# Attention and gated FFN in one kernel: the weighted-value products of a group's second half in the next group's first step, a seventh probsT slot, task 2 after the fourth tile's scores

## The reference, cut to what matters

```python
qkv = jnp.einsum('bsd,ed->bse', x, w_qkv) + b_qkv
scores = jnp.einsum('bhqd,bhkd->bhqk', q, k) / math.sqrt(Hd)     # Hd = 32
attn = jax.nn.softmax(scores + causal[None, None], axis=-1)
out = jnp.einsum('bhqk,bhkd->bhqd', attn, v)
x = _layernorm(x + jnp.einsum('bsd,ed->bse', out, w_out) + b_out)
h = jax.nn.silu(g) * u        # g, u: products with (gate_w - 128) * scale, (up_w - 128) * scale
x = _layernorm(x + jnp.einsum('bsi,hi->bsh', h, Wd))
```

## Time and profile before

| what | us |
|---|---|
| median of 3 runs (lowest, highest) | 754.64 (753.57, 755.45) |
| the profiled execution | 754.66 |
| its span, first to last instruction | 752.6 |
| PE, PEld, DVE, ACT, POOL busy | 730.2, 563.9, 392.5, 381.4, 135.5 |
| groups 0 and earlier, to 47.66 | PE busy 43.30 |
| FFN, 388.90 to 752.60 | PE busy 354.15 of 363.70 |

### The profile page before, as it was taken

The page is one execution under the profiler, slowest core; times in us unless marked ns, Lnnn a source line. Parts: engine busy times, 40 slices in busy tenths (PEclk is TensorE's granted clock), DMA queues, the critical chain, the costliest instruction groups (busy, mean ns, idle before and its releaser), DMA issues.

```text
span 752.6 us, 11957 instructions
## 1 busy us (share of the span) xinstructions
PE 730.2 (97%) x4480; PEld 563.9 (75%) x4480; DVE 392.5 (52%) x1004; ACT 381.4 (51%) x912; POOL 135.5 (18%) x154
## 2 busy tenths in 40 slices
PE   7999899999999999999899999999999999999994
PEld 6776576776777777776588888888888888888883
DVE  4756665666666665676653222643227332453335
ACT  3656766667766667766656555322223232322220
POOL 0010110304313061311816212230000000000003
PEclk9999999999999999999999999999999999999998
DMA  9201413334613355221587974541110010000201
GB/s 314 106 2 29 141 57 84 84 86 92 189 57 85 84 139 155 63 67 57 99 166 159 196 223 139 169 147 50 70 57 0 14 73 24 0 1 28 84 1 57
DMA packets 59463, 68.67 MB, mean 91 GB/s; under 512 B 33552, under 2 KB 35600, under 8 KB 59280
## 3 DMA queue, kind: packets, MB, share of 16 engines
q1 hardware_dynamic: 52880, 48.00, 21.3%
q0 software_dynamic: 6528, 19.93, 11.5%
HBM read 59.53 MB, written 14.68 MB: 99 GB/s over the span
## 4 chain that ended last, share of the span: by engine, by line
PE 89%; DVE 5%; ACT 4%; POOL 1%; issue 1%; DMA 1%; POOLq 0%; SPq 0%; DVEq 0%
PE bank L1438 15%; PE bank L1439 15%; PE bank L1220 12%; PE bank L1296 9%; PE bank L1445 7%; PE bank L1446 7%; PE bank L1235 6%; PE bank L1279 5%; PE bank L1317 5%; PE bank L1254 4%; ACT probs L757 2%; DVE probs L973 2%; PE bank L1328 1%; PE bank L1182 1%; ACT xT_hi L750 1%; PE bank L1192 1%
## 5 line engine op out<-in xcount | busy, mean ns | idle before, releaser
L757 ACT ACTIVATE probs<-probs,neg_max 128x128 f32<-128x128 f32 (+3 forms) x256 | 140.4, 552 | 12.0 <-DVE neg_max L973 11.9
L1089 DVE SCALAR_TENSOR_TENSOR hid<-bank,u_scale,silu 128x512 f32<-128x512 f32 x64 | 48.0, 750 | 164.3 <-PE bank L1439 163.1
L973 DVE CUSTOM_DVE_ANT_0 probs<-bank,causal 128x128 f32<-128x128 f32 (+3 forms) x256 | 111.6, 484 | 32.6 <-PE bank L1279 32.6
L1438 PE MATMUL bank<-xT_hi,gateT 128*128 128x512 f32 x256 | 100.3, 392 | 0.0
L1439 PE MATMUL bank<-xT_lo,gateT 128*128 128x512 f32 x256 | 99.7, 389 | 0.0
L1438 PE MATMUL bank<-xT_hi,upT 128*128 128x512 f32 x256 | 99.6, 389 | 0.0
L1439 PE MATMUL bank<-xT_lo,upT 128*128 128x512 f32 x256 | 99.6, 389 | 0.0
L865 ACT ACTIVATE silu<-bank,g_scale 128x512 f32<-128x512 f32 x64 | 44.0, 688 | 96.8 <-PE bank L1439 96.8
L1296 PEld LDWEIGHTS bank<-ident,probs 128*128 128x128 f32 x640 | 72.4, 140 | 27.1 <-issue 14.4
L871 ACT ACTIVATE hid_hi<-hid 128x512 fp32r<-128x512 f32 x58 | 36.7, 632 | 108.9 <-DVE hid L1089 108.9
L1445 PE MATMUL bank<-downT,hid_hi 128*128 128x512 f32 x232 | 90.3, 389 | 0.1
(11 more groups left out here) (102 smaller groups left out, 1185.6 us busy)
## 6 DMA issues: line engine op xcount, KB each, us to landing
scan_buf<-in_L_ffn_gate_w_dram SPq DMA_DIRECT2D x4, 1024.0 KB, 5.4
scan_buf<-in_L_ffn_up_w_dram SPq DMA_DIRECT2D x4, 1024.0 KB, 5.2
scan_buf<-in_L_ffn_down_w_dram SPq DMA_DIRECT2D x4, 1024.0 KB, 5.3
x_tok<-y_scratch SPq DMA_DIRECT2D x4, 1024.0 KB, 5.7
w_int<-in_L_ffn_gate_w_dram POOLq DMA_DIRECT2D x16, 256.0 KB, 3.4
w_int<-in_L_ffn_up_w_dram POOLq DMA_DIRECT2D x16, 256.0 KB, 3.1
w_int<-in_L_ffn_down_w_dram POOLq DMA_DIRECT2D x16, 256.0 KB, 3.9
z_tok<-y_scratch SPq DMA_DIRECT2D x4, 1024.0 KB, 5.7
```

What stands on the lines that cost most here:

```text
L757: nc.scalar.activation(probs[qb][:, j, :], probs[qb][:, j, :], ACT.Exp, bias=neg_max[:, qb, j:j + 1], scale=-1.0, accum_out=row_sum[:, qb, ...
L973: nc.vector.tensor_tensor_reduce(out=probs[qb][:, j, :], in0=score[j][:, first:first + w], in1=causal[:, S - w:S], scale=-SCALE, scalar=-F ...
L1089: nc.vector.scalar_tensor_tensor(out=hid[:, i % 2, :], in0=bank[:, :], scalar=u_scale[:, i:i + 1], in1=silu[:, i % 2, :], op0=ALU.mult, op ...
L1438: nc.tensor.matmul(acc[n][:, :], w[:, c, cols], form(xT_hi[:, c, :]), start=c == 0, stop=False)
```

## The change

Three numbers of two tables, and one size:

```diff
-    TASK_STEPS = [0, 0, 2, 8, 8, 10, 10, 12, 12, 15]
+    TASK_STEPS = [0, 0, 3, 8, 8, 10, 10, 12, 12, 15]
...
-    PRODUCT_STEPS = [8, 8, 12, 12, STEPS, STEPS]
+    PRODUCT_STEPS = [8, 8, STEPS, STEPS, STEPS, STEPS]
...
-    SLOTS = 6
+    SLOTS = 7
```

## The result

| what | before | after |
|---|---|---|
| median of 6 runs (lowest, highest), us | 755.03 (753.48, 755.45) | 748.67 (748.46, 749.80) |
| the profiled execution | 754.66 | 748.73 |
| its span | 752.6 | 746.8 |
| FFN, from its first product to the end | 363.7 | 363.7 |

The ratio is 0.9923, with a 95% interval of 0.9912 to 0.9933: 5.8 us faster (the two medians stand 6.4 apart). The prediction said 751.5, 3.2 us faster, and a range down to 749.5. So the sign was right, and the forecast had little more than half of the size. Two later measurements of the same kernel gave 0.9938 (0.9919 to 0.9956) and 0.9935 (0.9920 to 0.9949).

A forecast was written before the change was run, and what follows sets the result against it. PE's own queue was taken to set the end in most groups. Gains and losses by group summed to 3.2 us, taking 754.66 to 751.5, with a range of 749.5 to 753.7.

The forecast's parts named there:

- The stall of k: Step 12: k's first product waits for DVE's drain of q's bank and loses 0.31 (other bounds: nothing, 0.16).
- rival A: No stall at k: DVE's drain is no limit, 13 groups gain 0.31 more, 4.0 us, 747.5; chance 0.08.
- The waits of 0.3: Sign in the changed kernel's profile: PE waits of about 0.3 for DVE's q_sb, 12 of them, and one for v_tok.
- Task 2 in plain groups: Task 2 behind the scores: from the last product to the second product 2.1 instead of 2.17, 0.05 saved.
- The plain groups together: Nine groups (3, 4, 5, 7, 8, 9, 11, 12, 13) save 0.11 each, 1.0 in all.
- Groups 6 and 10: x1 gets its own bank, 0.7 earlier; the output projection waits some 0.3; net 0.25, with the products 0.3 saved each.
- Group 1: Around the inverse: the burst hidden ahead of it lies open behind it, +0.86, less 0.2 twice: 0.4 lost.
- Group 0: v stalls as k does elsewhere, but m = 5's wait of 0.21 for v gets cover: 0.4 saved in the sum.
- Groups 2 and 14: In 2, task 2's transposes and copy leave the chain to step 8, 1.0; in 14, ACT's x work earlier, 0.7.
- group 15: Task 2 no longer fits into the scores' wait for DVE, 0.4 lost; the burst gives 0.29: 0.1 lost.
- B: Only the steady gains come; chains of groups 2 and 14 find another last wait: 1.4 us, 753.3; chance 0.22.
- C: Slower: ACT's copy of task 2 holds tile 3's exponentials in step 3; 0.4 lost per group, 757.9; chance 0.04.

The follow-up runs named there:

- the kernel without the stall: Changed kernel with task 8 moved from step 12 to step 13, so k takes the bank task 6 left: 745.80 us, ratio 0.9888.
- task 2 alone: Kernel before with only task 2 moved behind the scores of tile 3, products and six buffers as before: 751.76 us, ratio 0.9961.
- products alone: Kernel before with only the products moved to the next step 0 and the seventh buffer, task 2 still ahead of the scores: 752.22 us, ratio 0.9968.
- m = 2 in step 12: Changed kernel with the products m = 2 put back in step 12, m = 3 staying in the next step 0: 750.41 us, ratio 0.9948.

## Why the prediction was wrong in size

**What bounds the kernel, and what the products cost (right in kind).** PE's queue set the end, and the burst given back in step 0 measured 0.86 as in the prediction, 1.65 - 0.79. (The prediction's "round" is four records, 0.22 long; what the description of the kernel calls one round of 8 records is two of these.)

**The stall of k (right as a mechanism, 0.1 too long).** The first step that failed is the choice among 0, 0.16 and 0.31. I took 0.31 "as it is the same sequence"; it was the same sequence of instructions, but not of waits. The stall was 1.24 - 1.02 = 0.22: the middle bound, 0.16, and 0.055 of restart. With task 9 coming 0.02 to 0.05 later than its term (1.47, which was read at a first product of q, not of k), step 12 took 2.73 to 2.76, not 2.80. Plain groups gained 0.08 to 0.15 from the products where 0.06 was said. The waits of 0.3 that I wanted as proof are not in the list of waits; the starts alone show the stall. By the text's own test rival A would have held, and it did not: the kernel without the stall is 3 us faster still. The listed waits were the wrong test.

**Task 2 in plain groups** gave 0.04 where 0.05 was said.

**The plain groups together.** The two parts alone add up to 1.32 for the nine groups (predicted 1.0), the changed kernel has 1.52. A group is about 21.79 or 21.83 long there, and which of them it is changes from profile to profile of the same kernel. 0.03 of the step lies between k's first product and task 9: 1.49 in the short groups, 1.52 in the long ones. What makes it is not traced.

**Groups 6 and 10 (the x part right, the rest left out).** Up to the scores in step 8 they are 0.31 and 0.33 shorter; less the 0.04 of every plain group that is the "net 0.25" of the prediction. What it lacked is that 0.04, 0.04 more from the products, and 0.10 to 0.15 in step 10: the transposes of tasks 5 and 6 followed the product ahead by 0.51 before, by 0.39 with task 2 moved. I had not looked past step 8. There task 5 takes the bank of task 3 and waits for DVE's copy of it; in both kernels it starts 0.05 behind the end of that copy, and the copy comes earlier with the rest of DVE's queue. Neither is a listed wait. Kernel before, then task 2 alone, timelines of DVE and PE in order of time, group 10:

```profile
270.01 0.69 DVE L479 COPY probsT<-bank 128x512 f32<-128x512 f32 x1
...
270.24 0.40 PE L1220 MATMUL bank<-xT_lo,wT_hi 128*128 128x512 f32 x1
...
270.75 1.09 PE L1296 MATMUL bank<-ident,probs 128*128 128x128 f32 x8
```

```profile
267.89 0.69 DVE L479 COPY probsT<-bank 128x512 f32<-128x512 f32 x1
...
268.24 0.40 PE L1220 MATMUL bank<-xT_lo,wT_hi 128*128 128x512 f32 x1
...
268.63 1.09 PE L1296 MATMUL bank<-ident,probs 128*128 128x128 f32 x8
```

**Group 1 (products right, task 2 missed).** The products cost 0.51 alone, near the "+0.86" less 0.4. But the term had nothing for task 2, which gave 0.38. Ahead of the scores in step 8 the product behind w11, q's first of group 3, follows it by 0.35 instead of 0.68, which is no listed wait either. That product needs w10's low part from DVE. Before, this ended 0.14 ahead of it, last in a chain that starts on ACT: task 2's copy, the high part of w12, its low part on DVE, the maxima of tile 3, w10's low part. Without the copy at its head the high part of w12 comes 0.48 earlier after the group's mark, w10's low part does too, and the wait is gone. It is the mechanism that the prediction had for group 2, and left out here. That task 2 and w12 exchange banks plays no part in this chain. Kernel before, then after, timelines of ACT, DVE and PE in order of time:

```profile
53.32 0.58 ACT L809 ACTIVATE probsT<-bank 128x512 f32<-128x512 f32 x1
...
54.31 0.58 ACT L743 ACTIVATE wT_hi<-bank 128x512 fp32r<-128x512 f32 x1
...
58.63 0.69 DVE L945 TENSOR_TENSOR wT_lo<-bank,wT_hi 128x512 fp32r<-128x512 f32 x1
...
58.78 0.60 PE L1182 MATMUL bank<-ident,w_stage 128*128 128x128 f32 x4
...
59.46 0.47 PE L1220 MATMUL bank<-xT_hi,wT_hi 128*128 128x512 f32 x1
```

```profile
52.41 0.58 ACT L743 ACTIVATE wT_hi<-bank 128x512 fp32r<-128x512 f32 x1
...
56.73 0.69 DVE L945 TENSOR_TENSOR wT_lo<-bank,wT_hi 128x512 fp32r<-128x512 f32 x1
...
57.33 0.60 PE L1182 MATMUL bank<-ident,w_stage 128*128 128x128 f32 x4
...
57.68 0.48 PE L1220 MATMUL bank<-xT_hi,wT_hi 128*128 128x512 f32 x1
```

**Group 0** gained 0.58, not 0.4: m = 5's wait was read as its listed 0.21, but by the starts it was 0.42: from the burst to the scores it is 1.21 there (47.66 to 48.87) and 0.79 in the earlier trace rows.

**Groups 2 and 14** came as said (1.04, 0.75), and **group 15** 0.18 better: the burst gave 0.26 as said (0.29), and task 2 cost 0.17, not 0.4. That only half of its four transposes shows is not traced.

**Sum.** The misses are all one way: plain groups 0.5, groups 6 and 10 0.5, group 1 0.3, groups 0 and 15 0.2 each: 1.7, so 3.2 became 4.9. The stall is about 0.5 of these 1.7 (0.4 in the plain groups, the rest in groups 2, 6 and 10, by the products alone); most of the others are terms put at nothing, task 2 in group 1 (0.38) and step 10 of groups 6 and 10 (0.25) above all. The other 0.9 of the measured 5.8 is the start. The range ended at 749.5, with the stall as the only term that could be better. It left out how the start scatters (2 us between profiles) and that each wait read from the list was a lower bound.

**Rivals.** A fell: the stall is there. B fell: the chains of groups 2 and 14 gave what was said. C fell: in task 2 alone no group but 15 is longer.

**The two rules.** The Trainium skill, page TensorEngine Tiling (Array Packing), section Key Properties, by which alone the prediction made some 6 us, comes close to the 5.8 by chance: the products, to which it was applied, are worth 1.8, and with k's stall taken away (3.1 more) still less than 6. The same page's section PSUM Bottleneck was borne out as a warning only: with the burst gone k's product waits for the drain of its bank and follows it by 0.055 in every group. That bank was filled by full-array products, not by the tiled ones of which the section speaks.

## What to carry to other kernels

Read a stall from the starts of the instructions around it. The listed idle time counts from a modelled end, and gave 0, 0.21 and 0 where the starts had 0.22, 0.42 and 0.33. Where banks go out by "whose last use ended first", list the bank of each job after the change before costing it: the stall of k and the best version (3 us for one step) hung on who takes q's bank. And where a job leaves the queue of one engine, follow the chain that stood behind it in every group: the miss in group 1 was such a chain. Before pricing a change below 1%, know how much a second profile of the same kernel differs, and where.

## What the runs showed of the hardware

- PE's first product behind a drain started 0.055 us after the end of DVE's instruction where it waited on one semaphore and 0.147 after it where it waited on two, one of them long satisfied: 24 cases in two kernels, each within 0.002. A part of this 0.09 was not lost: what followed came 0.03 to 0.07 sooner.
- A burst of quarter-array matmuls between full-array transposes and products cost 0.32 beyond its rounds: 0.18 to enter, 0.14 to leave (m = 2 in step 12).
- Behind two waits of 1.0, with 1.1 of transposes between them, the granted clock was at 0.50 for 3.4 us in some executions (3 of 12 profiles) and not in others of the same kernel. It cost 1.5 to 1.6 us. A shorter group with the same waits, 20.64 against 21.40, was no safer: one of three profiles in either kernel.
- TensorE began every profiled execution at the low level: the first transposes of all twelve were 0.21 apart, later ones 0.11. In 3 of 12 profiles some of the first products ran 0.427 apart, which is 512 columns at 1.2 GHz. The full level came between 6.9 and 12.2 us into the span, and up to then the view's 1.00 stands for a missing record.
